# Graph attention score stage: which wait the gathers carry, and where ScalarE normalises the src rows

## The reference

```python
h = jnp.maximum(_layernorm(x, axis=-1), 0.0)
residual = h
Q = (h @ Wq).reshape(n, H, D)      # H = 8 heads, D = 32
K = (h @ Wk).reshape(n, H, D)
V = (h @ Wv).reshape(n, H, D)
scores = jnp.einsum('ehd,ehd->eh', Q[dst], K[src]) * SCALE
attn_max = jnp.zeros((n, H), scores.dtype).at[dst].max(scores)
w = jnp.exp(scores - attn_max[dst])
attn_sum = jnp.zeros((n, H), w.dtype).at[dst].add(w)
w = w / (attn_sum[dst] + 1e-08)
msg = V[src] * w[:, :, None]
out = jnp.zeros((n, H, D), msg.dtype).at[dst].add(msg)
out = _layernorm(residual + out.reshape(n, OUT_DIM) @ Wo_w + Wo_b, ln1_g, ln1_b)
ffn = jax.nn.gelu(out @ ffn_w1 + ffn_b1, approximate=False) @ ffn_w2 + ffn_b2
out = _layernorm(out + ffn, ln2_g, ln2_b)
x = x + out
```

## Time and profile before

| | us |
|---|---|
| median of 3 runs | 1744.41 |
| lowest and highest run | 1738.28, 1752.1 |
| the profiled execution, its own time | 1733.5 |
| its span from the first to the last instruction | 1731.6 |
| TensorE busy | 1622.8 (94%) |
| VectorE busy | 1513.1 (87%) |
| ScalarE busy | 1318.5 (76%) |
| GpSimd busy | 1268.1 (73%) |

### The profile page before, as it was taken

The page is one execution under the profiler, slowest core; times in us unless marked ns, Lnnn a source line. Parts: engine busy times, 40 slices in busy tenths (PEclk is TensorE's granted clock), DMA queues, the critical chain, the costliest instruction groups (busy, mean ns, idle before and its releaser), DMA issues.

```text
span 1731.6 us, 31120 instructions
## 1 busy us (share of the span) xinstructions
PE 1622.8 (94%) x10389; PEld 1458.0 (84%) x10389; DVE 1513.1 (87%) x4615; ACT 1318.5 (76%) x2419; POOL 1268.1 (73%) x1281
## 2 busy tenths in 40 slices
PE   3887888998888999999999999999999999999997
PEld 2877777875667999999999999999999999999997
DVE  2676677978855999999999999999999999999996
ACT  1565667764465888888888888888888888888884
POOL 6465555426667888888888888888888888888883
PEclk7999899999999999999999999999999999999999
DMA  5588577525426777777777777777777777777761
GB/s 166 207 298 298 197 269 271 175 69 170 116 105 111 176 171 175 169 182 174 177 174 169 179 174 178 177 171 175 167 183 173 179 174 170 178 173 178 175 131 68
DMA packets 95281, 303.92 MB, mean 176 GB/s; under 512 B 16236, under 2 KB 21834, under 8 KB 95120
## 3 DMA queue, kind: packets, MB, share of 16 engines
q0 software_dynamic: 42336, 138.54, 39.8%
q1 hardware_dynamic: 52784, 163.38, 27.1%
HBM read 134.61 MB, written 118.53 MB: 146 GB/s over the span
## 4 chain that ended last, share of the span: by engine, by line
PE 68%; POOL 1%; DMA 0%; DVE 0%; issue 0%; ACT 0%; POOLq 0%; DVEq 0%; ACTq 0%
PE banks L966 32%; PE banks L955 30%; PE banks L941 5%; DMA vt<-agg_scratch 0%; ACT vt L1163 0%; POOL d_zx_rstd L1279 0%; DVE d_y_stats L1081 0%; POOL vt L1264 0%; POOL agg_scratch L1227 0%; DVE d_act_lo L1041 0%; POOLq L1324 0%; POOL vt L1266 0%; DMA agg_scratch<-c_rows,c_row_of 0%; DVE banks L1060 0%; POOL vt L1253 0%
## 5 line engine op out<-in xcount | busy, mean ns | idle before, releaser
L966 PE MATMUL banks<-d_w_hi,d_act_hi 128*128 128x256 f32 x1564 | 457.6, 293 | 0.0
L966 PE MATMUL banks<-d_w_lo,d_act_hi 128*128 128x256 f32 x1564 | 441.9, 283 | 0.0
L966 PE MATMUL banks<-d_w_hi,d_act_lo 128*128 128x256 f32 x1564 | 441.4, 282 | 0.0
L1163 ACT ACTIVATE vt<-vt,d_zx_nmr,d_zx_rstd 128x256 f32<-128x256 f32 x391 | 222.7, 594 | 145.7 <-POOL d_zx_nmr L1282 145.7
L955 PE MATMUL banks<-d_zt_hi,d_w_hi 128*128 128x512 f32 (+1 forms) x784 | 306.2, 391 | 4.6 <-DVE d_zt_lo L1048 2.7
L955 PE MATMUL banks<-d_zt_lo,d_w_hi 128*128 128x512 f32 (+1 forms) x784 | 305.8, 390 | 0.0
L955 PE MATMUL banks<-d_zt_hi,d_w_lo 128*128 128x512 f32 (+1 forms) x784 | 304.9, 389 | 0.0
L966 PEld LDWEIGHTS banks<-d_w_hi,d_act_lo 128*128 128x128 f32 x1564 | 298.8, 191 | 0.0
L966 PEld LDWEIGHTS banks<-d_w_hi,d_act_hi 128*128 128x128 f32 x1564 | 298.4, 191 | 0.1
L966 PEld LDWEIGHTS banks<-d_w_lo,d_act_hi 128*128 128x128 f32 x1564 | 298.0, 191 | 0.0
L1264 POOL TENSOR_TENSOR vt<-vt,d_g_row 128x1024 f32<-128x1024 f32 x98 | 288.7, 2946 | 2.9 <-ACT vt L1163 2.9
(11 more groups left out here) (167 smaller groups left out, 3606.4 us busy)
## 6 DMA issues: line engine op xcount, KB each, us to landing
agg_scratch<-vt SPq DMA_DIRECT2D x100, 512.0 KB
vt<-in_x SPq DMA_DIRECT2D x97, 512.0 KB
vt<-agg_scratch POOLq DMA_DIRECT2D x97, 512.0 KB, 5.5
vt<-vt POOLq DMA_DIRECT2D x97, 512.0 KB, 7.5
out<-vt SPq DMA_DIRECT2D x97, 512.0 KB, 2.9
a_xd<-in_x,a_idx POOLq DMA_INDIRECT x98
a_xs<-in_x,a_idx POOLq DMA_INDIRECT x98
score_scratch<-a_score SPq DMA_DIRECT2D x98, 4.0 KB
```

The lines of the kernel that those rows point to most:

```text
L966: ins = nc.tensor.matmul(Y[s % 2][:, j, :], a[:, c, j * P:(j + 1) * P], w[:, c, :], start=False, stop=(c == KF - 1 and w is w2_lo), skip_g ...
L1163: ins = nc.scalar.activation(zn[gz % 2][:, j, :], z[gz % ZR][:, j, :], ACT.Identity, bias=zx_nmr[:, at % NR, 0, j:j + 1], scale=zx_rstd[:, ...
```

## The change

Two places of the score stage are written in another order; no instruction that computes or moves data is added or taken away.

```diff
             for g in range(EG):
                 for n in range(2 * GT):
                     side, j = n // GT, n % GT
                     if j >= edge_blocks(g):
                         continue
-                    if g >= XG and j == 0:
-                        pool.wait_ge(h_done[side], g + 1 - XG)
                     if g >= XG + 1 and n == 0:
                         pool.wait_ge(v_done, KD * (g - XG - 1) + 1)
                     if g >= XG and n == GT:
                         pool.wait_ge(q_done, 2 * (g - XG) + 1)
+                    if g >= XG and j == 0:
+                        pool.wait_ge(h_done[side], g + 1 - XG)
...
             for s in range(FIRST, EG):
+                if 0 <= s < AHEAD:
+                    normalise(s + 1, 1, (0, 1))
                 key_copy(s, 0)
-                if s == -1 or s >= AHEAD:
+                if s >= -1:
                     normalise(s + 1, 1, (2, 3))
                 key_copy(s, 1)
                 high_part(s + 1, 0)
-                if 0 <= s < AHEAD:
-                    normalise(s + 1, 1, (0, 1, 2, 3))
```

## The result

The changed kernel takes **1721.4 us** (median of 5 runs, 1718.2 to 1725.2) where the kernel before, run beside it, takes 1738.3 (5 runs, 1737.6 to 1752.1): ratio **0.9873, 95% interval 0.9851 to 0.9896**, faster by 1.3%. The forecast was 1736, its range began at 1723.

What follows compares the result with a forecast made beforehand. GpSimd's gathers with held TensorE events were taken to set 13.2 to 13.5 us a step; after the change 22 x (12.42 + 0.35), 3.0 and 22.5 give 306.4 us against 314, so 1736 us, range 1723 to 1753.

Steps and rivals of the forecast that it cites:

- The loop of 12.42 us: Score stage: ScalarE and VectorE from one `a_nmr` to the next, with src rows ahead of K's copies, become the bound.
- GpSimd's loop: Score stage: two runs of gathers and two gaps a step, 13.2 us before, forecast to fall to 12.2.
- The gathers' wait, 0.49 us a run,: GpSimd in the score stage: letting the gather carry its wait for TensorE's event saves 0.49 us a run.
- The rival that it does nothing: A carried wait starts at 0.76 us, GpSimd's loop stays at 13.2 us; 2 us more, 1746 us, chance 0.22.
- The term of 0.35 us a step for the src transposes' event: Score stage: event held behind the dst run of gathers delays the src high and low parts, 0.35 us a step average.
- the prediction's own bound: Score stage with nothing for held events: 298.7 us, 15 less than before.
- The base: Whole kernel: the median of 1744.41 us before the change, from which the saving of 8 us was taken.
- The last two steps: End of the score stage, steps without gathers: 11.8 and 10.7 us, 22.5 in the sum.
- the exponentials' 3.0: ScalarE behind step 15: table load and computing, with part of a second load, stand on the path, 3.0 us once.
- Holding ends altogether: Rival: TensorE's events are held only by GpSimd's separate wait; all steps 12.4 us, about 1727 us, chance 0.17.
- ScalarE's part is slower than what it replaces: Rival: VectorE's chain waits behind K's copies, src rows and held events; 14.1 us a step, 1766 us, chance 0.08.
- its own late step of 10.8 us: Score stage before the change: a step where the ScalarE and VectorE loop took 10.8 us, read as not the bound.

Runs made afterwards that it cites:

- the hold: Sets of runs where TensorE's events come 0.5 us and more behind their matmul beside GpSimd's gathers; kernel before 1735 to 1741 us, without it 1649 to 1650.
- run 4: Changed kernel with the second pair of src rows moved behind K's copies and the dst high parts; 1719.3 us, ratio 0.9879.
- Run 1: Kernel before with the gathers' part of the change alone, ScalarE in its old order; 1727.4 us, ratio 0.9924.
- run 17: Kernel before with the gathers' part alone, in a set without the hold; 1649.7 us, ratio 1.0000.
- run 14: Kernel before, unchanged, run for its trace in a set without the hold; 1648.6 us.
- run 13: Changed kernel, unchanged, in a set without the hold; 1678.6 us, ratio 1.0171 against the kernel before.
- run 16: Changed kernel with a wait for TensorE's next event at each run's third gather too, with the hold; 1721.2 us beside 1741.2 of the kernel before.
- run 8: Changed kernel, but the src run of gathers waits for Q's event in a separate instruction again; without the hold, 1678.6 us, ratio 1.0179.
- run 9: Kernel before, unchanged, run for its trace in a set with the hold; 1735.1 us, ratio 0.9993.
- run 15: Changed kernel with a wait for TensorE's next event at each run's third gather too, without the hold; 1677.4 us.
- Run 3: Changed kernel without any wait of GpSimd for TensorE's events, with the hold; 1771.9 us, ratio 1.0195.

## Why the prediction was wrong

**The loop of 12.42 us** was right as a sum: 12.24 was measured where nothing else binds, so the addition from rows of the old order came within 0.2 us. Without the hold this loop is the bound. With it GpSimd's loop of 12.3 to 12.4 us lies beside it, so that the 12.34 of the changed kernel, which fits the forecast too, is in part luck: run 4, whose own loop of ScalarE and VectorE is 11.38, has the same steps.

**The gathers' wait, 0.49 us a run,** was right for its size. Gathers start 0.26 us behind TensorE's event where they started 0.76 behind, the gaps shrank from 1.9 to 1.4, GpSimd's loop from 13.2 to 12.35 (forecast 12.2). Run 1 shows it alone at 0.992. The rival that it does nothing fell there; without the hold it does nothing (1.0000), for another reason, since nobody waits for GpSimd: most steps are 10.9 to 11.0 us in run 17 as in run 14.

**The term of 0.35 us a step for the src transposes' event** is the step that failed. The places were right: the transposes end 8.2 us behind `a_nmr` as forecast, inside a dst run (109.98, in a run from 106.67 to 111.37). The hold was not there: `a_hts_hi` starts 0.04 us later, and VectorE's `a_hts_lo` never waited for it. With nothing in its place the stage is 298.7 us by the prediction's own bound; measured 299.0. The term was 7.7 us of 22 steps, and its absence is half of the miss.

The trace of before had the answer. The hold of the earlier trace rows is from a step in which two runs had joined: the dst run began 0.53 us behind a src run, so that the transposes ended over the last part of eight gathers.

```profile
135.99 0.95 POOL L174 DMA_INDIRECT a_xs<-in_x,a_idx  x1 [0.30 <-issue]
137.47 0.94 POOL L174 DMA_INDIRECT a_xd<-in_x,a_idx  x1 [0.53 <-issue]
```

In the step of the earlier trace rows the src transposes end at 103.12 (102.03 + 1.09), inside a dst run that stands alone and ends at 104.06, and ScalarE takes the event at once:

```profile
103.16 1.08 ACT L306 CAST a_hts_hi<-banks 128x512 fp32r<-128x512 f32 x2 [0.22 <-issue]
```

So it is in all steps of the kernel before with a dst run that stands alone; this event is late only in steps in which two runs had joined. In the profile after no dst run joins a src run, and with that the case that the term was taken from is gone.

**The base** is most of the other half. The saving was taken from 1744.41, the median of three runs; beside the changed kernel five runs have 1738.34. 1738.3 less 15.4 (314.1 - 298.7) is 1723, and 1721.4 was measured. That the profiled execution came to 1725.21 where 1725.5 was forecast for it is luck: the stage saved 7 us more than forecast, and the message stage of that execution lost as much.

**The smaller terms** held. The last two steps took 12.2 and 10.3 us from Q to Q, 22.5 together as forecast; the exponentials' 3.0 were 2.3 in the step itself, with and without the hold. The step two later was 1.1 longer than its neighbours, which runs 13 and 16 do not show, so it is no price of theirs.

**The rivals.** "Holding ends altogether" gave the steps that came (12.4, 1727 us), but for a reason that fell: K's second event is still 2.2 us late in the changed kernel, and without the hold runs 8 and 14 have the separate wait and no late event (K's come 0.01 us behind their matmuls in run 14). Its second half held: TensorE's granted clock was 0.99 against 0.95, and the longest idle time between its matmuls from 60 to 300 us was 2.2 us against 4.2. That the one comes of the other no run shows. "ScalarE's part is slower than what it replaces" had 0.08 and needed a long hold in each step. What came true in run 13 needs no hold at all: where the kernel before runs below 12.24 us a step, the change is slower by the difference, up to 1.34 us. The prediction saw this in its own late step of 10.8 us and did not ask when that would be every step.

**What would have shown it.** From the earlier trace rows alone: 22 steps of 12.4 in place of 10.8 would be some 35 us more if the hold were absent (measured 27.7). The trace of before could not tell that it can be absent.

## What to carry to other kernels

A stall of TensorE that sits between the parts of a kernel's step can be absent in another set of runs of the same program (a stage of 312.6 us in run 9 and of 266.8 in run 14): before filling it with work moved from elsewhere, add up the loop that the move makes, and compare it with the steps in which the stall does not occur. Moving a wait so that a gather carries it cost nothing here where nobody waited for the gathers and saved 0.7% where somebody did, so of the two parts it is the one to keep: the gathers' part alone was 0.992 and 0.994 with the hold and 1.000 without, the whole change 0.987 and 0.991 against 1.017. When a term rests on one row, look at the same event in the other steps of the trace before taking its size: the late event of the earlier trace rows was on time wherever the gathers stood as the change would put them. Take the time before from the runs made beside the changed kernel, and compare only within one set.

## What the runs showed of the hardware

**Beside GpSimd's rows of gathers TensorE is slowed in some sets of runs and not in others, with the same program.** It shows at the start, where TensorE runs matmuls that wait for nothing while GpSimd issues 28 gathers 0.30 us apart. Run 9, TensorE in order of time:

```profile
17.73 1.90 PE L380 MATMUL banks<-a_wq_hi 128*128 128x256 f32 x12
21.38 0.28 PE L380 MATMUL banks<-a_wq_hi 128*128 128x256 f32 x1 [1.74 <-issue]
23.47 0.37 PE L380 MATMUL banks<-a_wq_hi 128*128 128x256 f32 x1 [1.82 <-issue]
...
40.97 0.37 PE L410 MATMUL banks<-ident,a_hd 128*128 128x128 f32 x1 [1.02 <-issue]
```

Run 14, the same kernel:

```profile
17.75 3.40 PE L380 MATMUL banks<-a_wq_hi 128*128 128x256 f32 x27
21.11 1.09 PE L410 MATMUL banks<-ident,a_hd 128*128 128x128 f32 x8
21.96 2.40 PE L380 MATMUL banks<-a_wq_hi 128*128 128x256 f32 x18
```

In run 9 the matmuls come one by one, with up to 2.43 us of idle between them. The row of gathers ends at 38.2 us; from then on the idle shrinks to 1.0 us, and from 42.4 us on there is none. The first of Q starts at 47.5 us. In run 14 the longest idle time there is 1.32 us, and it starts at 26.5. The difference of the two spans, 1728.3 and 1646.8, is 81.5 us: 21.0 before Q's first matmul, 45.8 in the score stage, and most of the rest in the message stage, whose scatters are DMA_INDIRECT rows on GpSimd like the gathers (146.5 us from the first to the last against 132.0). From the last scatter to the end it is 1212 us in both.

What decides between the two is open. All runs of one set were of one kind. The record numbers the chips: 3 and 7 with the hold, 13 and 8 without, but number 1 stands both beside runs 13 to 15 (without) and beside run 16 (with). So the expectation that it belongs to the chip fell, unless a number doesn't name one piece. By what path the gathers reach TensorE is open too. That the matmuls of the first 40 us wait for no semaphore, and come late all the same, says that it is not only events that are held; in the score stage matmuls mostly kept their pace while events came late (in the profile after V's run from 104.75 on, while K's event is out). Run 3 has longer rows and later events; run 16 shows that an event due in a run's first gather passes. The runs with half of the gathers all fell in sets without the hold, so that it is the gathers and not something else of that time that slow TensorE rests on their place in time, and on run 3.

**The time by which TensorE's event is late,** where it is, ends in the profile after, in four of five late events on record, 1.0 to 1.3 us behind the last of a run's gathers; so it does elsewhere (128.82 and 130.00 in run 4, 92.72 and 93.9 in run 16, 97.42 and 98.46 in the earlier trace rows). In the kernel before, where runs join, it is more scattered, up to 2.1 us behind, and the earlier trace rows has 1.69. Without the hold the events of run 14 come 0.01 us behind their matmuls. No run shows what makes up the 2.2 us by which K's second event is late in the runs with the hold.
